# One written list of all steps, each with its own banks, in place of a list that repeats for each sequence

## The chip, the cores and the metric

The kernel runs on one core of one Trainium2 chip. The time is that of the device in microseconds, from one launch; of several runs the median is given. The core's engines are TensorE (PE, with its weight loads as PEld), VectorE (DVE), ScalarE (ACT), GpSimd (POOL) and SyncE (SP), which only issues DMAs here. Each works through its own queue in order, and they meet at semaphores.

## The reference

One layer of a hybrid network on 16 sequences of 256 tokens with 128 channels, in fp32. Four blocks follow one another, each on the normalised x and added to it:

```python
x = x + attn_a(_layernorm(x), ...)   # gated linear attention with decays by level, 32 heads of 64
x = x + ffn(_layernorm(x), ...)      # softmax attention, 16 heads of 8, then 8 experts of 256, the best 2 weighted
x = x + attn_b(_layernorm(x), ...)   # 9 sigmoid gates times v, shifted by 0, +-1, +-4, +-16, +-32 tokens
x = x + ffn(_layernorm(x), ...)      # the same weights as above
```

In attn_a an input projection gives z, x, B, C and small gates; a causal convolution of four taps and a silu follow; then `att = qk * decay * lam_ts`, where the level of a pair of tokens comes from a Fenwick tree; then the sum over tokens, the product with silu(z), an RMS norm and the output projection. No step of one sequence needs anything of another.

## The kernel before

All work is cut into steps. A step is a name, a layer (0, or 1 for the second ffn and the mixing block), a sequence n and a number k. The names in the order of one sequence: `gates` (layernorm, small gates, their running sums, the table of decays written to DRAM), `lvl` (39 loads that bring this table back), `conv`, `tap`, `taps`, `silu`, `xt`, `xcopy` (convolution: matmul, ACT's tap, DVE's three taps, silu, transposition, copy), `zgate`, `zact`, `qk`, `place`, `coef`; for each of eight units `weigh` (PE's log decays), `wexp` (their exponential on ACT), `prod` (times qk on DVE), `own` (POOL), `sum` (PE) and `gated` (DVE); `ssq` and `outp` (RMS and output projection). Then `fn`, `q`, `v`, `mload`, `smax`, `rowmax`, `maxt` (maxima of the scores, for which q and k are split in bf16 parts on POOL and go through DRAM), `sload`, `es`, `exps`, `ep`, `ocopy`, `tail` (scores, softmax, output, layernorm, expert choice), `up`, `relu`, `down`, `acc`, `experts` (the experts), `mix` (attn_b, k from 0 to 12), and `fn` to `experts` once more as layer 1.

The order is written by hand as text. `PERIOD` is one list of words, such as `up1.0+4@67`: step up, layer 1, k = 0, of the sequence that entered 4 turns ago, with PSUM banks 6 and 7. `order()` runs through the list once per turn, with 20 turns in all, so that up to five sequences are in work at once, and leaves out the sequences that don't exist; that is the fill in the first turns and the drain in the last. `build()` goes through the resulting list once per engine, in the blocks `sync`, `tensor`, `scalar`, `vector` and `gpsimd`; each takes the steps in which it has a part, in the order of the list, and waits on semaphores for what others must have done. A bank that is used again is waited for by the number of drains so far (`drained`), a filled one by `filled`; both numbers are counted from the list. So only the order within each engine counts, and what an engine does ahead of a step it doesn't take part in is of no account.

`order()` also sets ScalarE's tables. It walks the list of all steps and puts in a table load where the set changes:

```python
needed = ("silu_set" if what in SILU_SET else "exp_set" if step in EXP_SET.get(what, ()) else held)
if needed != held:
    hops.append((needed, 0, n, 0))
    held = needed
```

`SILU_SET` is silu, zact and mix; `EXP_SET` is some steps of gates, tail and outp, and all of wexp and exps. It goes by names, also for steps in which ACT has no part, such as `mix` 0 and `mix` 12 (k == NG + 3), which are VectorE's alone.

Lines that the text below names: L524 and L533 (SP: decay table out and back), L593 to L610 (gates on PE), L630 (conv and zgate), L653 (xt), L670 and L678 (weigh), L691 and L699 (sum), L710 (ssq), L724 (outp), L739 (fn), L765 (smax), L775 (maxt), L862 (up), L874 (down), L882 to L901 (mix), L916 and L918 (the table loads), L1003 (wexp), L1049 (exps), L1220 (taps), L1247 (prod), L1255 (gated), L1260 (w_out times norm_w, once, in the first sequence), L1295 (rowmax), L1379 (acc).

Of the kernel before, what the change touches and what calls it, by code (L numbers as in the profile page):

```python
# [122 lines left out]
PERIOD = """  # L123
up0.2+3@03 relu0.3+3 silu0.1+1 load_x0.0+0 ocopy1.3+4 up0.3+3@51 lvl0.0+1 lvl0.1+1 down0.2+3@7 experts1.3+5
conv0.2+1@32 ep1.3+4@4 conv0.3+1@65 down0.3+3@1 tap0.3+1 fn0.1+2@7 acc0.1+3 gates0.0+0 up0.5+3@34 acc0.2+3 xt0.0+1@7
silu0.2+1 conv0.4+1@13 taps0.2+1 acc0.3+3 taps0.3+1 relu0.5+3 up0.4+3@20 xcopy0.0+1 tap0.4+1 down0.5+3@7 lvl0.2+1
taps0.4+1 relu0.4+3 lvl0.3+1 lvl0.4+1 lvl0.5+1 tail1.0+4@54 xt0.1+1@2 xcopy0.1+1 q0.1+2@0 down0.4+3@6 acc0.4+3
tap0.5+1 conv0.5+1@24 relu0.6+3 up0.6+3@15 acc0.5+3 relu0.7+3 silu0.3+1 taps0.5+1 acc0.6+3 up0.7+3@61 q0.0+2@0
down0.6+3@3 down0.7+3@2 tail1.1+4@6 acc0.7+3 experts0.2+3 zgate0.0+1@71 tail1.2+4@0 silu0.4+1 v0.0+2@6 experts0.3+3
xt0.3+1@3 zact0.0+1 zgate0.6+1@05 zgate0.2+1@74 mix1.0+3 lvl0.6+1 xcopy0.3+1 zact0.6+1 zact0.2+1 silu0.5+1 tail1.3+4  # L130
xt0.2+1@2 conv0.6+1@75 xt0.4+1@0 conv0.7+1@43 mload0.0+2 tap0.6+1 xcopy0.2+1 xcopy0.4+1 tap0.7+1 mix1.1+3@12 taps0.6+1
place0.0+1@1 tail1.4+4@0 taps0.7+1 mix1.2+3@6 bcp0.0+1 mix1.3+3@2 mix1.4+3@5 mix1.5+3@1 rowmax0.0+2 zact0.5+1
zgate0.5+1@60 qk0.0+1@7 silu0.6+1 smax0.0+2@1524 mix1.6+3@3 qkc0.0+1 zact0.4+1 zgate0.4+1@01 mix1.7+3@6 tail1.5+4@3
rowmax0.1+2 smax0.1+2@7265 tail1.6+4 mix1.8+3@4 silu0.7+1 relu1.0+4 zact0.3+1 zgate0.3+1@30 mix1.9+3@1 taps0.8+1
up1.0+4@67 conv0.8+1@42 tap0.8+1 mix1.10+3@1 zgate0.7+1@06 zact0.7+1 xcopy0.6+1 rowmax0.2+2 xt0.6+1@7 experts1.0+4@5
zgate0.1+1@16 sload0.0+2 zact0.1+1 smax0.2+2@5740 lvl0.7+1 up1.1+4@16 relu1.1+4 experts1.1+4@2 mix1.11+3@7 rowmax0.3+2
xt0.5+1@5 xcopy0.5+1 down1.0+4@4 silu0.8+1 mix1.12+3 wexp0.0+1 smax0.3+2@3671 weigh0.0+1@02 wexp0.3+1 down1.1+4@5
weigh0.3+1@63 relu1.2+4 xt0.7+1@0 up1.2+4@27 maxt0.0+2@1 up1.3+4@32 gates0.1+0@7 down1.2+4@1 fn1.0+3 acc1.0+4
relu1.3+4 xcopy0.7+1 own0.0+1 acc1.1+4 wexp0.2+1 coef0.0+1 wexp0.1+1 exps0.0+2 prod0.0+1 weigh0.2+1@46 acc1.2+4
weigh0.1+1@25 gates0.2+0@37 es0.0+2@6412 sum0.0+1@0 fn1.1+3@7 prod0.1+1 own0.1+1 sum0.1+1@5 weigh0.4+1@3210 gated0.0+1  # L140
wexp0.4+1 ep0.0+2@6 own0.2+1 ocopy0.0+2 own0.3+1 own0.4+1 q1.0+3@4 es0.1+2@2571 exps0.1+2 own0.5+1 sum0.2+1@3 q1.1+3@0
up1.4+4@25 ep0.1+2@6 relu1.4+4 es0.2+2@0753 ocopy0.1+2 exps0.2+2 wexp0.5+1 mload1.0+3 sum0.3+1@2 prod0.2+1 gated0.1+1
weigh0.5+1@4615 own0.6+1 ep0.2+2@0 prod0.3+1 sload1.0+3 prod0.4+1 es0.3+2@3624 down1.3+4@7 own0.7+1 sum0.4+1@1
gated0.2+1 ocopy0.2+2 weigh0.6+1@5746 gates0.3+0 exps0.3+2 gated0.3+1 wexp0.6+1 prod0.5+1 acc1.3+4 ep0.3+2@2
down1.4+4@3 gates0.4+0@5 gates0.6+0 ocopy0.3+2 acc1.4+4 sum0.5+1@7 wexp0.7+1 weigh0.7+1@3065 gated0.4+1 prod0.6+1
gated0.5+1 tail0.0+2@24 up1.5+4@10 sum0.6+1@7 gates0.5+0 relu1.5+4 smax1.0+3@2563 prod0.7+1 tail0.1+2@4 sum0.7+1@0
gated0.6+1 rowmax1.0+3 cpart0.0+0 up1.6+4@27 tail0.2+2@4 smax1.1+3@1256 relu1.6+4 outp0.0+1@7 smax1.2+3@5146
ssq0.0+1@2 gated0.7+1 ssq0.1+1 ssq0.2+1 ssq0.3+1 smax1.3+3@0351 rowmax1.1+3 outp0.1+1 tail0.3+2 rowmax1.2+3
rowmax1.3+3 maxt1.0+3@6 tail0.4+2@4 acc1.5+4 outp0.2+1 down1.5+4@5 up0.0+2@40 down1.6+4@3 acc1.6+4 relu0.0+2 exps1.0+3
v1.0+3@2 fn0.0+1 relu1.7+4 es1.0+3@6137 up1.7+4@50 tail0.5+2@6 ep1.0+3@1 tail0.6+2 es1.1+3@6524 acc1.7+4 down1.7+4@3  # L150
exps1.1+3 conv0.0+0@05 tap0.0+0 taps0.0+0 up0.1+2@62 taps0.1+0 ocopy1.0+3 experts0.0+2@4 relu0.1+2 conv0.1+0@31
ep1.1+3@7 es1.2+3@4520 tap0.1+0 down0.1+2@6 ocopy1.1+3 experts0.1+2@7 ep1.2+3@5 es1.3+3@0712 exps1.2+3 experts1.2+4
ocopy1.2+3 exps1.3+3 acc0.0+2 relu0.2+2 down0.0+2@4 silu0.0+0 tap0.2+0
"""


START = """
# [6 lines left out]
def hop_words(text):  # L164
    for word in text.split():
        name, rest = word.split(".")
        step, n = rest.split("@")[0].split("+")
        yield name[:-1], int(name[-1]), int(step), int(n)


def hop_banks(text):
    for word in text.split():
        name, rest = word.split(".")
        if "@" in rest:
            yield (name[:-1], int(name[-1]), int(rest.split("+")[0])), tuple(int(b) for b in rest.split("@")[1])
# [1406 lines left out]
```

## Time and profile before

| | |
|---|---|
| median of 3 runs | 2107.03 us (2103.94 to 2107.87) |
| the profiled execution | 2103.15 us |
| its span, first to last instruction | 2101.4 us |
| PE, DVE, ACT, POOL busy | 1921.0, 1738.5, 1488.0, 775.6 us |
| mean granted TensorE clock | 0.966 of full speed |
| DMA | 117.14 MB, mean 56 GB/s |

The rows below come from that one execution, whose own time lies 3.9 us under the median of the three runs. A busy PE is not PE at its peak, since the ends of matmuls are modelled; an fp32 matmul shows as two records, and a weight load (PEld) runs beside the matmuls. "Idle before" is the time in which an engine had nothing running ahead of an instruction, with the engine, tile and line whose semaphore came last.

### The profile page before, as it was taken

How to read it: one execution, taken by the hardware profiler on the slowest of the kernel's cores; microseconds unless marked ns; L12 is line 12 of the kernel's file. 1: busy time of each engine (PE TensorE's matmuls, PEld its weight loads, DVE VectorE, ACT ScalarE, POOL GpSimd, SP SyncE). 2: the span in 40 equal slices, each digit the busy share in tenths (PEclk: the TensorE clock that was granted, in tenths of full speed). 3: DMA queues.
4: the chain of work that ended last, by engine and by line, in shares of the span. 5: the costliest groups of instructions: out<-in, count | busy, mean ns of one | idle time of the engine just before them, and what ended most of it. 6: DMA issues, size and time to landing. Idle time of an engine off the chain costs nothing.

```text
span 2101.4 us, 48245 instructions
## 1 busy us (share of the span) xinstructions
PE 1921.0 (91%) x16928; PEld 1491.0 (71%) x16928; DVE 1738.5 (83%) x4463; ACT 1488.0 (71%) x3207; POOL 775.6 (37%) x1139
## 2 busy tenths in 40 slices
PE   4779899999999999999999999999999999997757
PEld 3556677777877777786877778786777778774545
DVE  5776988989898988989898998989898898865643
ACT  4566768778686868778686877868686877855332
POOL 5313353525243343525244352424334352423120
PEclk8889999999999999999999999999999999998867
DMA  5021232211222222211222222121222221112110
GB/s 162 12 63 12 60 67 60 65 41 46 50 59 67 62 67 63 56 35 51 59 60 67 62 64 56 45 44 54 67 60 67 62 63 38 50 53 71 27 56 6
DMA packets 224576, 117.14 MB, mean 56 GB/s; under 512 B 124360, under 2 KB 210512, under 8 KB 219216
## 3 DMA queue, kind: packets, MB, share of 16 engines
q1 hardware_dynamic: 224336, 114.06, 21.5%
q8 instruction: 137, 2.24, 0.5%
q14 instruction: 103, 0.84, 0.1%
HBM read 67.60 MB, written 46.14 MB: 54 GB/s over the span
## 4 chain that ended last, share of the span: by engine, by line
PE 64%; DVE 23%; ACT 4%; issue 4%; SPq 2%; POOL 2%; DMA 1%; DVEq 0%; ACTq 0%; POOLq 0%
DVE nmax L1295 6%; PE psA L862 6%; PE psB L724 6%; DVE work L1220 5%; PE psB L874 5%; PE psA L874 5%; PE psA L699 5%; PE psB L803 3%; PE psB L862 3%; PE psA L630 3%; PE psB L699 2%; PE psA L803 2%; DVE att L1247 2%; DVE hid L1408 2%; PE psA L788 2%
## 5 line engine op out<-in xcount | busy, mean ns | idle before, releaser
L1247 DVE TENSOR_TENSOR att<-att,QK 128x1024 f32<-128x1024 f32 x192 | 251.2, 1341 | 15.2 <-ACT att L1003 15.1
L1529 POOL TENSOR_TENSOR own<-X,ccoef 128x512 f32<-128x512 f32 x128 | 160.2, 1257 | 206.7 <-PE psA L699 97.1
L1437 POOL TENSOR_SCALAR var_eps<-lnmv 128x2 f32<-128x2 f32 x128 | 40.4, 316 | 524.0 <-DVE lnmv L1110 521.3
L1220 DVE SCALAR_TENSOR_TENSOR work<-psA,c_conv_w,work 128x255 f32<-128x255 f32 (+2 forms) x450 | 195.4, 474 | 11.8 <-ACT work L961 11.8
L630 PE MATMUL psA<-xnT_a,c_w_in 128*128 128x256 f32 x608 | 177.9, 397 | 17.8 <-DVE hid L1220 8.7
L1072 ACT ACTIVATE hid<-psA,c_b 128x256 f32<-128x256 f32 x295 | 135.8, 485 | 79.4 <-PE psA L862 79.2
L1295 DVE TENSOR_REDUCE nmax<-psB 128x2 f32<-128x512 f32 x288 | 186.6, 680 | 1.1 <-PE psB L765 1.1
L862 PE MATMUL psA<-x1T,c_w 128*128 128x256 f32 x608 | 178.9, 394 | 1.5 <-DVE nmax L1295 1.3
L1049 ACT ACTIVATE pt<-psB 128x512 f32<-128x512 f32 x256 | 147.4, 614 | 31.5 <-PE psB L789 31.4
L1295 DVE TENSOR_REDUCE nmax<-psA 128x2 f32<-128x512 f32 x224 | 149.8, 681 | 15.1 <-PE psA L765 14.9
L1220 DVE SCALAR_TENSOR_TENSOR work<-psB,c_conv_w,work 128x255 f32<-128x255 f32 (+1 forms) x360 | 159.0, 474 | 2.7 <-ACT work L961 2.1
L874 PE MATMUL psB<-c_w,hid 128*128 128x128 f32 x1152 | 160.6, 285 | 0.4 <-ACT hid L1072 0.4
L874 PEld LDWEIGHTS psB<-c_w,hid 128*128 128x128 f32 x1152 | 148.3, 199 | 8.8 <-issue 4.2
L1519 POOL TENSOR_TENSOR O_sb<-O_sb,hid 128x256 f32<-128x256 f32 x128 | 98.8, 772 | 148.8 <-DVE hid L1408 141.6
L1049 ACT ACTIVATE pt<-psA 128x512 f32<-128x512 f32 x256 | 150.3, 618 | 0.1
L1379 DVE SCALAR_TENSOR_TENSOR ff<-psB,w_e,ff 128x128 f32<-128x128 f32 x288 | 86.8, 342 | 73.1 <-PE psB L874 71.4
L630 PE MATMUL psB<-xnT_a,c_w_in 128*128 128x256 f32 x480 | 137.9, 392 | 0.8 <-ACT hid L1072 0.7
L862 PE MATMUL psB<-x1T,c_w 128*128 128x256 f32 x416 | 125.3, 396 | 13.0 <-DVE nmax L1295 11.9
L630 PEld LDWEIGHTS psA<-xnT_a,c_w_in 128*128 128x128 f32 x608 | 107.3, 196 | 39.6 <-DVE hid L1220 10.3
L1003 ACT ACTIVATE att<-psA 128x512 f32<-128x512 f32 x176 | 96.6, 599 | 53.4 <-PE psA L670 51.9
L1003 ACT ACTIVATE att<-psB 128x512 f32<-128x512 f32 x208 | 114.9, 603 | 21.6 <-PE psB L670 18.8
L724 PE MATMUL psB<-c_w_out,Z 128*128 128x128 f32 x1024 | 124.3, 280 | 3.8 <-DVE c_w_out L1260 3.8
(326 smaller groups left out, 5375.3 us busy)
## 6 DMA issues: line engine op xcount, KB each, us to landing
qk_scr<-kparts SPq DMA_DIRECT2D x96, 192.0 KB, 2.4
k_stack<-qk_scr SPq DMA_DIRECT2D x32, 576.0 KB
q_stack<-qk_scr SPq DMA_DIRECT2D x32, 576.0 KB
qk_scr<-qparts SPq DMA_DIRECT2D x96, 128.0 KB, 1.9
k_max<-qk_scr SPq DMA_DIRECT2D x128, 64.0 KB, 2.0
q_max<-qk_scr SPq DMA_DIRECT2D x128, 64.0 KB, 2.0
lvl_scr<-work SPq DMA_DIRECT2D x32, 192.0 KB, 5.7
qk_scr<-qparts SPq DMA_DIRECT2D x96, 64.0 KB, 1.7
```

Source lines behind the costliest of these rows:

```text
L630: e.matmul(t[:, 0:T], w_in[:, first + j * P:first + (j + 1) * P], xnT_a[:, :], start=True, stop=True).then_inc(filled[b], 1)
L699: m = e.matmul(t[j * HD:(j + 1) * HD, f * P:(f + 1) * P], X[:, s, fc + j * HD:fc + (j + 1) * HD], att[:, 2 * f + j, :], start=False, stop= ...
L724: m = e.matmul(t[:, k * P:(k + 1) * P], Z[:, f, k * P:(k + 1) * P], w_out[:, f, :], start=(f == 0), stop=(f == NF - 1))
L862: e.matmul(t[:, 0:T], w_1[:, k, j * P:(j + 1) * P], x1T_b[lay][:, :], start=True, stop=True).then_inc(filled[b], 1)
L874: m = e.matmul(t[:, i * P:(i + 1) * P], hb[:, j, i * P:(i + 1) * P], w_2[:, 2 * k + j, :], start=(j == 0), stop=(j == 1))
L1003: e.activation(att[:, :, c:c + 64], t[:, :].rearrange("p (t h) -> p h t", h=HG), ACT.Exp).then_inc(drained[b], 1)
L1049: e.activation(pt_b[a % PTS][:, :, :].rearrange("p h q -> p (h q)"), t[:, :], ACT.Exp, scale=float(AD) ** -0.5).then_inc(drained[b], 1)
L1072: e.activation(hid_b[lay][k % 2][:, j, :], t[:, 0:T], ACT.Relu, bias=b_1[:, 2 * k + j:2 * k + j + 1]).then_inc(drained[b], 1)
L1220: m = e.scalar_tensor_tensor(out=cv[:, back:], in0=t[:, 0:T - back], scalar=conv_w[:, c, tap:tap + 1], in1=cv[:, back:], op0=ALU.mult, op1 ...
L1247: e.tensor_tensor(att[:, :, :], att[:, :, :], bc(QK[:, kq, :], 1, HG), ALU.mult).then_inc(att_done, 1)
L1295: e.tensor_reduce(nmax[:, i, p0:p0 + 2], t[:, :].rearrange("p (h k) -> p h k", k=T), AX.X, ALU.max).then_inc(drained[b], 1)
L1529: e.tensor_tensor(own_b[k % 2][:, :].rearrange("p (h c) -> p h c", c=HD), X[:, tt, h0 * HD:(h0 + HG) * HD].rearrange("p (h c) -> p h c", c ...
```

## The change

`PERIOD` and the empty `START` are replaced by `ORDER`, a text of all steps of all sequences in one order, each word with its sequence and its own banks. `order()` no longer unrolls turns; it reads the words and puts in the table loads by the same rule as before. The order within each engine is another one from place to place, in all turns, and so are the banks. Five waits are added for what the old order had made certain: PE ahead of the output projection (the gated sums of this half of the tokens), PE ahead of the first `up` of a layer (its input, transposed x1), DVE ahead of a gated sum (both gate tiles), DVE ahead of `rowmax` (the maxima of the layer before are taken) and POOL ahead of `own` (both copied tiles). No instruction of the computation is another one.

```diff
-PERIOD = """
-up0.2+3@03 relu0.3+3 silu0.1+1 load_x0.0+0 ocopy1.3+4 up0.3+3@51 lvl0.0+1 lvl0.1+1 down0.2+3@7 experts1.3+5
...
-"""
-START = """
-"""
+ORDER = """
+load_x0.0.0 gates0.0.0 gates0.1.0@0 gates0.2.0@12 conv0.0.0@34 gates0.3.0 tap0.0.0 gates0.4.0@5 gates0.5.0 taps0.0.0 conv0.2.0@67 cpart0.0.0
...
+wexp0.0.8 down1.0.5@3 xcopy0.7.8 weigh0.3.8@21 xt0.7.8@7 relu1.2.5 rowmax0.3.7 mix1.12.6 up1.2.5@56 up1.3.5@74 wexp0.3.8 maxt0.0.7@5 relu1.3.5
...
+"""
 def hop_words(text):
     for word in text.split():
-        name, rest = word.split(".")
-        step, n = rest.split("@")[0].split("+")
-        yield name[:-1], int(name[-1]), int(step), int(n)
+        name, step, rest = word.split(".")
+        n, _, used = rest.partition("@")
+        yield (name[:-1], int(name[-1]), int(n), int(step)), tuple(int(b) for b in used)
-def hop_banks(text):
...
 def order():
-    period = list(hop_words(PERIOD))
...
-    for turn in range(BATCH + max(lag for _, _, _, lag in period)):
-        runs += [(what, lay, turn - lag, step) for what, lay, step, lag in period
-                 if 0 <= turn - lag < BATCH and (what, lay, turn - lag, step) not in ahead]
     hops, held = [], "exp_set"
-    for what, lay, n, step in runs:
+    for hop, _ in hop_words(ORDER):
+        what, _, n, step = hop
         needed = ("silu_set" if what in SILU_SET else "exp_set" if step in EXP_SET.get(what, ()) else held)
...
+        first_up = {}
+        for hop in hops:
+            if hop[0] == "up":
+                first_up.setdefault(hop[1:3], hop)
...
 PE, outp, k < NT
+                    e.wait_ge(*empty(("sum", 0, n, NU // 2 * (k + 1) - 1)))
 PE, up
+                    if hop == first_up[lay, n]:
+                        e.wait_ge(*empty(("tail", lay, n, 4)))
 DVE, gated, tt == 0
+                        e.wait_ge(*empty(("zgate", 0, n, 2 * hg), 1))
 DVE, rowmax
+                    if nth[hop]:
+                        e.wait_ge(nmax_ready, nth[hop])
 POOL, own, tt == 0
+                        e.wait_ge(*empty(("xt", 0, n, 2 * hg)))
```

## Rows read from the trace of the kernel before

**Rows 1.** The page, part 1: busy us, share of the span and instructions of each engine.

```profile
PE 1921.0 (91%) x16928; PEld 1491.0 (71%) x16928; DVE 1738.5 (83%) x4463; ACT 1488.0 (71%) x3207; POOL 775.6 (37%) x1139
```

**Rows 2.** Windows: busy us (instructions) of PE, PEld, DVE, ACT, POOL; PEclk; DMA share; GB/s.

```profile
0.00:68.00 68.00, 34.90 (x144) 24.99 (x144) 40.68 (x106) 36.27 (x70) 31.01 (x40) 0.88 0.45 128
68.00:158.00 90.00, 67.97 (x554) 51.38 (x552) 68.53 (x147) 51.14 (x99) 22.59 (x33) 0.86 0.18 41
...
969.00:1000.00 31.00, 30.89 (x338) 21.91 (x337) 28.59 (x51) 28.42 (x60) 19.44 (x19) 1.00 0.10 30
1000.00:1020.00 20.00, 19.57 (x244) 15.63 (x244) 19.13 (x37) 9.28 (x18) 7.75 (x17) 1.00 0.57 123
974.00:1094.00 120.00, 116.42 (x1064) 91.78 (x1063) 108.02 (x280) 92.56 (x201) 47.76 (x72) 1.00 0.22 57
1811.00:1930.00 119.00, 106.40 (x965) 79.97 (x963) 78.28 (x201) 69.31 (x151) 39.56 (x56) 0.91 0.18 51
1930.00:2050.00 120.00, 81.11 (x549) 59.01 (x548) 59.75 (x175) 44.03 (x99) 25.11 (x42) 0.80 0.18 50
```

**Rows 3.** PE's waits, 497 to 1691 us: engine line waited for: total us, times, longest us.

```profile
PE psA L888 <- ACT srcT L1077: 14.1, 10, 1.4
PE psB L862 <- DVE nmax L1295: 7.7, 10, 0.8
PE psA L893 <- ACT hid L1091: 7.1, 10, 0.7
PE psB L691 <- DVE Z L1255: 4.3, 10, 0.4
```

**Rows 4.** PE's waits, 0 to 68 us.

```profile
PE psA L630 <- DVE hid L1220: 8.7, 2, 5.3
PE psB L608 <- DVE work L1194: 5.9, 1, 5.9
PE psA L670 <- DMA high<-lvl_scr: 3.1, 1, 3.1
```

**Rows 5.** PE's waits, 68 to 158 us.

```profile
PE psA L630 <- DVE work L1220: 5.2, 1, 5.2
PE psB L608 <- DVE work L1194: 3.9, 1, 3.9
PE psB L724 <- DVE c_w_out L1260: 3.8, 1, 3.8
PE psA L765 <- DMA q_max<-qk_scr: 3.1, 1, 3.1
```

**Rows 6.** Timeline, 100 to 127 us: start, us, what, [idle before <- releaser].

```profile
115.13 0.35 DVE L1266 SCALAR_TENSOR_TENSOR x<-psB,rms,x 128x128 f32<-128x128 f32 x1 [11.53 <-ACT rms L1023]
...
121.60 2.07 PE L630 MATMUL psA<-xnT_a,c_w_in 128*128 128x256 f32 x4 [5.20 <-DVE work L1220]
```

**Rows 7.** ACT's groups: xcount | busy us, mean ns | idle before.

```profile
L918 ACT ACT_TABLE_LOAD x33 | 42.3, 1283 | 0.6
L916 ACT ACT_TABLE_LOAD x33 | 42.3, 1283 | 0.6
```

**Rows 8.** Timeline of ACT, 954 to 975 us.

```profile
956.38 1.28 ACT L916 ACT_TABLE_LOAD   x1
957.76 0.22 ACT L1061 ACTIVATE gate_e<-gate_l 128x16 f32<-128x16 f32 x1
957.99 1.28 ACT L918 ACT_TABLE_LOAD   x1
```

**Rows 9.** PE's waits, 1930 to 2101 us.

```profile
PE psA L765 <- DMA q_max<-qk_scr: 10.5, 2, 9.0
PE psB L765 <- DVE nmax L1295: 6.6, 6, 2.1
PE psB L775 <- DVE nmax_bf L1302: 6.6, 2, 3.3
```

**Rows 10.** All waits, the whole span.

```profile
PEld psA L699 <- issue: 13.4, 80, 0.2
```

More of the change, by code:

```diff
@@ L129 @@
[L129 to L138, printed above, removed]
@@ new lines @@
+weigh0.7.7@1574 own0.7.7 down1.4.4@0 tail0.0.6@36 wexp0.7.7 prod0.7.7 up1.5.4@15 sum0.6.7@7 relu1.5.4 gates0.5.8 smax1.0.5@4036 tail0.1.6@1
+rowmax1.0.5 gated0.5.7 gated0.6.7 cpart0.0.8 sum0.7.7@5 tail0.2.6@1 smax1.1.5@4036 up1.6.4@27 outp0.0.7@1 smax1.2.5@5403 gates0.6.8 ssq0.0.7@6
+gated0.7.7 ssq0.1.7 ssq0.2.7 relu1.6.4 ssq0.3.7 rowmax1.1.5 tail0.3.6 smax1.3.5@2754 lvl0.0.8 rowmax1.2.5 outp0.1.7 rowmax1.3.5 tail0.4.6@0
+maxt1.0.5@3 outp0.2.7 relu0.0.6 lvl0.1.8 acc1.5.4 fn0.0.7 exps1.0.5 v1.0.5@2 down1.6.4@7 up0.0.6@54 down1.5.4@6 es1.0.5@0315 tail0.5.6@4 up1.7.4@60
@@ new lines @@
+tail0.5.11@4 exps1.1.10 ep1.0.10@3 ocopy1.0.10 es1.1.10@5704 tap0.0.13 relu0.0.11 down1.7.9@2 tail0.6.11 conv0.0.13@57 relu0.1.11 up0.1.11@04
+ep1.1.10@3 acc1.7.9 experts0.0.11@2 taps0.0.13 conv0.1.13@61 ocopy1.1.10 down0.1.11@0 es1.2.10@4253 tap0.1.13 exps1.2.10 taps0.1.13 experts1.2.9
+lvl0.3.13 experts0.1.11@7 es1.3.10@4265 exps1.3.10 acc0.0.11 relu0.2.11 ep1.2.10@1 down0.0.11@3 tap0.2.13 ocopy1.2.10 silu0.0.13 gates0.0.14
+up0.2.11@42 silu0.1.13 conv0.2.13@76 conv0.3.13@53 acc0.1.11 down0.2.11@4 up0.3.11@20 experts1.3.9 relu0.3.11 ep1.3.10@1 xt0.0.13@7 tap0.3.13
@@ new lines @@
+tap0.6.13 zgate0.0.13@25 zact0.2.13 zgate0.6.13@43 tail1.3.10 silu0.5.13 zgate0.2.13@02 conv0.7.13@50 tap0.7.13 mload0.0.12 mix1.1.11@22
+zgate0.4.13@61 zact0.6.13 taps0.6.13 tail1.4.10@2 xcopy0.3.13 taps0.7.13 mix1.2.11@4 mix1.3.11@3 xt0.4.13@2 xcopy0.4.13 lvl0.5.13 mix1.4.11@7
+bcp0.0.13 mix1.5.11@4 zact0.5.13 zgate0.5.13@53 silu0.6.13 rowmax0.0.12 smax0.0.12@0274 mix1.6.11@5 mix1.7.11@3 zact0.4.13 silu0.7.13 zact0.3.13
+zgate0.3.13@05 smax0.1.12@3267 tail1.5.10@1 lvl0.6.13 rowmax0.1.12 xt0.6.13@4 tail1.6.10 up1.0.10@01 mix1.8.11@5 qk0.0.13@3 relu1.0.10 mix1.9.11@2
@@ new lines @@
+smax1.0.13@7164 gated0.7.15 sum0.7.15@3 smax1.1.13@5027 rowmax1.1.13 tail0.1.14@1 up1.6.12@64 tail0.2.14@1 v1.0.13@3 outp0.0.15@5 smax1.2.13@6402
+relu1.6.12 ssq0.0.15@7 own0.7.15 tail0.3.14 ssq0.1.15 rowmax1.2.13 sload1.0.13 ssq0.2.15 ssq0.3.15 smax1.3.13@1364 rowmax1.3.13 outp0.1.15
+tail0.4.14@0 maxt1.0.13@2 relu0.0.14 outp0.2.15 down1.5.12@1 up0.0.14@36 acc1.5.12 exps1.0.13 relu1.7.12 tail0.5.14@4 down1.6.12@7 es1.0.13@0251
+up1.7.12@36 exps1.1.13 fn0.0.15 es1.1.13@4072 ep1.0.13@5 up0.1.14@13 acc1.6.12 tail0.6.14 down1.7.12@6 experts0.0.14@4 ep1.1.13@0 fn0.1.15@7
@@ L165, in hop_words @@
     for word in text.split():
-        name, rest = word.split(".")
-        step, n = rest.split("@")[0].split("+")
-        yield name[:-1], int(name[-1]), int(step), int(n)
-def hop_banks(text):
[L172 to L175, printed above, removed]
-def order():
-    period = list(hop_words(PERIOD))
-    runs = [(what, lay, n, step) for what, lay, step, n in hop_words(START) if n < BATCH]
-    ahead = set(runs)
-    for turn in range(BATCH + max(lag for _, _, _, lag in period)):
-        runs += [(what, lay, turn - lag, step) for what, lay, step, lag in period
-                 if 0 <= turn - lag < BATCH and (what, lay, turn - lag, step) not in ahead]
+        name, step, rest = word.split(".")
+        n, _, used = rest.partition("@")
+        yield (name[:-1], int(name[-1]), int(n), int(step)), tuple(int(b) for b in used)
+def order():
     hops, held = [], "exp_set"
-    for what, lay, n, step in runs:
+    for hop, _ in hop_words(ORDER):
+        what, _, n, step = hop
         needed = ("silu_set" if what in SILU_SET else "exp_set" if step in EXP_SET.get(what, ()) else held)
@@ L190, in order @@
             held = needed
-        hops.append((what, lay, n, step))
+        hops.append(hop)
     return hops
@@ L197, in build @@
     hops = order()
-    banks = dict(hop_banks(PERIOD))
+    banks = dict(hop_words(ORDER))
     bank_at, nth, uses, seen_hops = {}, {}, [0] * 8, {}
     for hop in hops:
-        for j, b in enumerate(banks.get((hop[0], hop[1], hop[3]), ())):
+        for j, b in enumerate(banks.get(hop, ())):
             bank_at[hop, j] = (b, uses[b])
```

385 lines of the change are left out of this document (366 added, 19 removed).

## The prediction, made before the changed kernel ran

> **What bounds the kernel now.** I read the busy times first: PE works 1921 us of 2101, DVE 1738, ACT 1488 [rows 1]. A share over the whole span hides that the program has three stretches, so next comes the table of windows, cut where a new sequence enters the pipeline [rows 2]. In the middle, from about 377 to 1811 us, a new sequence enters every 119 to 120 us, 12 times; in the turn at 974 to 1094 us PE is busy 116.42 of 120 us at full clock, DVE 108.02, ACT 92.56. While the pipeline fills, PE is busy 34.90 of 68 us and 67.97 of 90 us, with a granted clock of 0.88 and 0.86. While it drains, PE is busy 106.40 of 119 and 81.11 of 120, at 0.91 and 0.80. So PE's own queue sets the time in the middle, and chains through several engines set it at both ends.
>
> Then PE's waits, stretch by stretch. In the ten turns from 497 to 1691 us they sum to 33 us in four rows: 1.4 us in each turn inside the first matmul of the mixing stage (a transpose, ACT's copy, the next matmul, all in one step), 0.8 us for a bank held by a row maximum, 0.7 us for a tanh, 0.4 us for a gated sum [rows 3]. The 1.4 us lie within one step, and no order of steps removes them. What another order can remove is 3.6 - 1.4, some 2.2 us a turn, 26 us over 12 turns. In the fill it is 8.7 us for bank drains by the convolution taps, 5.9 us for the gates and 3.1 us for the decay table [rows 4]; then 5.2, 3.9, 3.8 and 3.1 us in the second stretch [rows 5]. The last two sequences pay 10.5 us for the loads of q_max and 6.6 and 6.6 us for row maxima [rows 9].
>
> **What the change is, by counting in the two lists.** The steps are the same 4928 (16 times the 308 words of the period), with 3840 bank uses in both, so every engine runs the same instructions apart from ACT's table loads. It is no new pipeline: the PE work listed ahead of each stage of each sequence is moved by 1.2 us on average and by 18 at most, the lists weighed with the trace's PE durations. On each engine steps have moved by 1.5 places on average on PE (at most 26, of 2288), 1.7 on ACT, 0.8 on DVE, 0.4 on GpSimd, 1.1 on SP. Nearly every bank is another one: 163 of 2224 steps that use banks keep theirs.
>
> **Fill: -9 us.** The first 65 us don't shrink. The first decay tile waits for 39 loads that SP issues one after another, and PE waits for the last of them 3.1 us [rows 4]; the taps' 8.7 us and the gates' 5.9 us lie ahead of that wait, so filling them with later gate matmuls, as the list does, moves no end. But two steps of PE that stood behind the wait (a transpose and the next sequence's first) now stand ahead of it, some 1.8 us less afterwards. From 68 to 158 us the list acts on things that wait. Of the next sequence's convolution, two pairs are now ahead of the output projection, where PE idles 3.8 us until DVE has scaled w_out [rows 5], and one group of taps is ahead of DVE's output step, where DVE idles 11.53 us for the rms [rows 6]. That group is six instructions of 0.47 us, 2.4 us, and it comes off DVE's queue behind 115 us, where PE waits 5.20 us for the group that follows it [rows 6]. The running sum for the next sequence's gates stands one gated sum later in DVE's queue and one sum later in PE's, which takes up part of the 3.9 us [rows 5]. I take 2 us before 68, 6 of the 16 us of waits up to 158, and 1 from the following turns together. Bounds: 0 and 18.
>
> **Middle: -5 us.** The bank that the first expert matmul of the second layer takes was last used by a row maximum (0.8 us a turn [rows 3]); in the new list both of its banks come from other kinds of step in 9 of 16 turns, and the sum that waited for the gated sum ahead of it takes another kind's bank in 14. Against that, 2061 new banks and some 115 PE steps moved by more than 5 places bring waits of their own where a reuse is now closer. I take a net gain of 0.4 us a turn times 12, of the 2.2 that are there. Bounds: -26 us if they all go, and +18 us if each turn gains 1.5 us of new waits, as much as the two largest removable ones of rows 3 together.
>
> **Table loads: 0 on the path, 38.5 us of ACT.** The program that reads the list puts a load of the silu set ahead of each step named mix, and step 12 of mix is one, though only DVE has work in it. In the old list it stands ahead of the first exponential of the decay tiles. In the new one it stands behind it, for 14 sequences, and once more at the end: ACT then loads silu and, right after, exp again for nothing. Counted with the program's rule that is 96 loads in place of 66. A load is 1283 ns [rows 7], and the step behind it starts 0.1 us after its end: 956.38 + 1.28 = 957.66 against 957.76 [rows 8]. A pair therefore costs 2.57 us, 15 pairs 38.5 us. Queued behind a pair are three exponentials, two relus, then the first softmax exponentials and the gates' own, for which DVE's products and PE's sums wait. ACT is busy 28.42 of 31 us from 969 to 1000 us and 9.28 of 20 after [rows 2]: 2.58 us of idle time in the tight part, about one pair, and 10.7 us behind it. So a pair is worked off before the next sequence's stages, and I take 0; at most it is 2.57 us in each turn.
>
> The Trainium skill speaks against such an order: "ScalarE: Activation LUTs", Rules for kernel authors, says to do all of one table set before switching, and What ACT_TABLE_LOAD costs puts a switch at 1283 ns for the load and 1380 ns for a drain, 2.66 us. The trace agrees with the load and not with the drain, which these rows don't show. By the page's price the 30 loads would be an estimated 80 us of ACT in place of 38.5, and its idle time could not hide that.
>
> **The five waits: +1 us.** PE waits for two gated sums ahead of the output projection (32 instructions) and for the transposed x1 ahead of the first expert matmul of a layer (32). Behind each waits all of PE's queue; both were done before by the order. DVE's wait for the maxima of the layer before, DVE's second wait on the gate tiles and GpSimd's on the copied x are for things done on the same queue or pairs of the same stage. What a wait costs where it is long fulfilled, no row shows by itself. The nearest is the weight load that starts late with nothing to wait for, 13.4 us for 80, 0.17 us each [rows 10]: 64 of them would be 11 us. The matmuls ahead still run then, so nothing is the other end; I take 1 us, nearer to that end.
>
> **Drain: -6 us.** The longest wait, 9.0 us for q_max [rows 9], is a chain of GpSimd's splits and DMAs. The new list starts k ahead of q and puts about as much expert work in between as before, so most of it stays; 1 us. Behind it, in the score matmuls and ahead of the transposition of the maxima, PE waits 6.6 and 6.6 us [rows 9]; there the list puts a down step more for sequence 14, an up and a down step for 15, and I take 3 of the 13 us. In the last 36 us four up steps stand ahead of the expert weights' transposition, which fills the gap there, 2 us. Bounds: 0 and 20.
>
> **The sum.** -9 - 5 + 0 + 1 - 6 = -19 us. The profiled run took 2103.15 us, its span is 2101.4; 2103.15 - 19 = 2084. The median of the runs, 2107.03, lies 3.9 us above the profiled run, so I name 2088 for a median.
>
> **The rivals.**
> ACT's table loads decide (slower). Place: between the first and second exponential group of each turn, where ACT has 2.58 us to spare in 31 us and DVE 2.4 [rows 2]. If the idle time lies ahead of what waits and not behind it, each pair is paid in full: 14 times 2.57 is 36 us, less about 15 of the gains above, 2107 + 21 = 2128; paid by half, 2110. It decides from the point where a pair is delayed by more than what PE still has queued ahead of the sums, under 2 us. For it: three engines over 90% busy there. Against it: the idle time behind. The skill's rule on grouping by table set is this case.
> New waits by banks eat the gain: 1.5 us in 12 turns is 18 us, 2107. For it: DVE has 12 us a turn to spare, so a late step is not soon made up. The order does what it says and the time stands still.
> The list removes nearly all it can: 26 in the middle, 14 in the fill, 10 in the drain, 2057. Against it: most of the ends are chains of one sequence, which no order shortens.
> The list does not act at all, since the ends were bound by DMAs and the middle by PE's work: 2107 with 3 us either way.
>
> **How the numbers follow.** Forecast 0.50 (2070 to 2100), nearly all removed 0.16 (2057), new bank waits 0.13 (2100 to 2115), table loads 0.16 (2108 to 2128), no effect 0.05. Faster takes the first two, 0.66; within 0.2%, about what a measurement of this kernel tells from no change, 0.10 from the bank waits and no effect; slower 0.24. The range 2050 to 2125 leaves out the far ends of the two outer cases.
>
> **What the new profile would show.** 96 table loads, two with no activation in between behind the first exponentials. PE idle of 68 to 158 us down from 22 to about 16; the wait of 5.2 us gone. PE's waits in a middle turn at 2 to 4 us, with other releasers than row maxima. If a new sequence enters every 119 us and the ends are each some 7 us shorter, the steps are right. If the turn is over 120.5 us and PE waits for the exponentials of the decay tiles or DVE's products, the table loads were underrated. If the waits are spread over many banks, it is the second rival. Wrong it would be above all by the middle, where 1 us a turn counts for 12.

## The result, and the profile of the changed kernel

| | before | after |
|---|---|---|
| median of the runs | 2105.49 us (4 runs, 2103.29 to 2107.87) | 2136.39 us (4 runs, 2126.58 to 2142.73) |
| ratio | | 1.0141, 95% interval 1.0120 to 1.0162: slower |
| profiled execution, its span | 2103.15, 2101.4 us | 2126.58, 2124.8 us |

The forecast was 2088 us and faster. The time is 2136 us, slower, and above the range of 2050 to 2125. The profiled execution of after is the fastest of its four, so the rows below show 23 us of loss (2124.8 against 2101.4) and not the 31 us of the medians.

The first part of the page, and the row of TensorE's granted clock over 40 slices of the span, answer to [rows 1]:

```profile
PE 1942.0 (91%) x16928; PEld 1496.2 (70%) x16928; DVE 1747.3 (82%) x4463; ACT 1517.3 (71%) x3237; POOL 792.0 (37%) x1139
PEclk9899999999999999999999999999999999998987
```

ACT has 30 instructions more, the table loads, and is busy 29.3 us longer. PE has the same 16928 matmuls and is busy 21 us longer. That is the first thing to explain: where the same matmuls take longer, the clock is the suspect. Over the whole span it can't be, for the mean granted clock is 0.971 in this execution and 0.966 in that of before; in single stretches it can. The windows (columns as in [rows 2]): the stretch from the second to the third sequence, the same 90 us as in [rows 2], two turns of the middle, and the last but one stretch of 120 us:

```profile
59.00:151.00 92.00, 73.59 (x584) 51.72 (x584) 71.33 (x158) 59.65 (x116) 22.57 (x35) 0.89 0.19 42
68.00:158.00 90.00, 75.31 (x618) 53.45 (x618) 74.40 (x155) 59.39 (x115) 24.26 (x36) 0.91 0.19 41
981.00:1105.00 124.00, 119.03 (x1068) 92.89 (x1068) 108.98 (x280) 95.71 (x206) 47.81 (x70) 0.99 0.22 54
1105.00:1231.00 126.00, 119.30 (x1068) 93.47 (x1068) 111.32 (x286) 97.35 (x208) 53.02 (x74) 0.99 0.23 55
1959.00:2079.00 120.00, 86.12 (x584) 61.17 (x582) 59.78 (x182) 48.60 (x109) 26.20 (x43) 0.85 0.18 50
```

A turn takes 124 and 126 us where it took 120, and its clock is 0.99 where it was 1.00. To see where the time comes from I mark one matmul, the first of each sequence's gates, and note its start in both traces (us):

| sequence | 1 | 2 | 3 | 5 | 7 | 9 | 11 | 13 | 15 | mixing stage of 15 |
|---|---|---|---|---|---|---|---|---|---|---|
| before | 68 | 158 | 260 | 497 | 736 | 974 | 1213 | 1453 | 1691 | 1993 |
| after | 59 | 151 | 251 | 496 | 737 | 981 | 1231 | 1480 | 1722 | 2028 |

The fill gains 9 us by the fourth sequence (number 3), as forecast. The mark of sequence 1 (59 against 68) shows no gain by itself: the new list puts this step ahead of the first decay tile, and that tile starts at 66.1 us against 65.4. Then 40 us are lost in the middle, in turns of 119.5 to 127.6 us that were all 119.4 to 119.8. From the mixing stage of the last sequence to the end the new list gains again.

PE's waits from 496 to 1722 us, ten turns like those of [rows 3], the six largest:

```profile
PE psA L1234 <- ACT srcT L1423: 10.7, 7, 2.2
PE psA L951 <- DVE work L1540: 5.0, 4, 1.6
PE psB L951 <- DVE work L1540: 4.9, 5, 1.3
PE psB L1234 <- ACT srcT L1423: 3.5, 3, 1.6
PE psA L1132 <- DMA q_stack<-maxT: 2.6, 2, 1.9
PE psA L1220 <- ACT att L1349: 2.2, 1, 2.2
```

The in-step wait of the mixing stage is still there (10.7 + 3.5 us, line 1234 is 888 of before). The row maximum of [rows 3] (7.7 us) is gone, as is the gated sum (4.3). New are the fourth gate step (L951, 9.9 us in nine turns), a DMA, and waits for `att`, the exponentials of the decay tiles. One of the latter, in the timelines of ACT and PE (start, us, what, [idle before <- releaser]), and the clock right behind it:

```profile
979.77 1.01 ACT L1418 ACTIVATE hid<-psB,c_b 128x256 f32<-128x256 f32 x2
980.80 1.28 ACT L1264 ACT_TABLE_LOAD   x1
982.09 1.28 ACT L1262 ACT_TABLE_LOAD   x1
983.38 1.08 ACT L1349 ACTIVATE att<-psA 128x512 f32<-128x512 f32 x2
984.03 1.16 PE L1220 MATMUL psA<-c_w,hid 128*128 128x128 f32 x8 [2.23 <-ACT att L1349]
985.70:989.10 3.40, 3.40 (x16) 1.71 (x13) 0.51 (x2) 2.06 (x4) 0.34 (x1) 0.50 0.01 2
```

Two loads with nothing between them, the exponential behind them, and an expert matmul that waits 2.23 us because its bank is drained by that exponential. Then the granted clock is 0.50, the lower of its two levels (1.2 GHz), for 3.4 us in which PE is busy all the time. Such a stretch at half the clock does 1.7 us of work in 3.4. Before shows none between 275 and 1790 us; after shows five of 3.4 us and one of 6.8 in the middle. So there are three suspects for the middle: the 15 pairs of loads, waits of the new order or its banks, and the clock behind either.

### The profile page after: what moved, and what is told of

It is laid out like the page before. It is cut to its first block and busy times, and to the rows that moved or that the text cites. A ratio compares the mean times of both kernels' runs of the same rounds, so it can differ in the third digit from the quotient of the medians.

```text
span 2124.8 us, 48449 instructions
## 1 busy us (share of the span) xinstructions
PE 1942.0 (91%) x16928; PEld 1496.2 (70%) x16928; DVE 1747.3 (82%) x4463; ACT 1517.3 (71%) x3237; POOL 792.0 (37%) x1139
## 5 line engine op out<-in xcount | busy, mean ns | idle before, releaser
L1593 DVE TENSOR_TENSOR att<-att,QK 128x1024 f32<-128x1024 f32 x192 | 262.8, 1403 | 21.8 <-ACT att L1349 20.8
L1566 DVE SCALAR_TENSOR_TENSOR work<-psA,c_conv_w,work 128x253 f32<-128x253 f32 (+2 forms) x414 | 185.3, 474 | 11.6 <-ACT work L1307 11.2
L1566 DVE SCALAR_TENSOR_TENSOR work<-psB,c_conv_w,work 128x253 f32<-128x253 f32 (+2 forms) x396 | 177.4, 473 | 5.7 <-ACT work L1307 5.5
L1208 PE MATMUL psB<-x1T,c_w 128*128 128x256 f32 x518 | 152.9, 396 | 3.2 <-ACT att L1349 1.9
L1418 ACT ACTIVATE hid<-psB,c_b 128x256 f32<-128x256 f32 x251 | 116.6, 484 | 52.3 <-PE psB L1208 43.9
L1208 PE MATMUL psA<-x1T,c_w 128*128 128x256 f32 x506 | 146.7, 391 | 2.7 <-ACT att L1349 1.2
L1220 PE MATMUL psA<-c_w,hid 128*128 128x128 f32 x1024 | 144.1, 286 | 5.4 <-ACT att L1349 2.2
L1220 PEld LDWEIGHTS psA<-c_w,hid 128*128 128x128 f32 x1024 | 131.3, 198 | 18.6 <-issue 8.7
L1418 ACT ACTIVATE hid<-psA,c_b 128x256 f32<-128x256 f32 x245 | 113.5, 488 | 41.6 <-PE psA L1208 36.7
L1220 PE MATMUL psB<-c_w,hid 128*128 128x128 f32 x1024 | 140.5, 282 | 1.3 <-ACT hid L1418 1.3
L1220 PEld LDWEIGHTS psB<-c_w,hid 128*128 128x128 f32 x1024 | 129.3, 195 | 13.2 <-issue 7.6
```

Source lines behind the costliest of these rows:

```text
L1208: e.matmul(t[:, 0:T], w_1[:, k, j * P:(j + 1) * P], x1T_b[lay][:, :], start=True, stop=True).then_inc(filled[b], 1)
L1220: m = e.matmul(t[:, i * P:(i + 1) * P], hb[:, j, i * P:(i + 1) * P], w_2[:, 2 * k + j, :], start=(j == 0), stop=(j == 1))
L1418: e.activation(hid_b[lay][k % 2][:, j, :], t[:, 0:T], ACT.Relu, bias=b_1[:, 2 * k + j:2 * k + j + 1]).then_inc(drained[b], 1)
L1566: m = e.scalar_tensor_tensor(out=cv[:, back:], in0=t[:, 0:T - back], scalar=conv_w[:, c, tap:tap + 1], in1=cv[:, back:], op0=ALU.mult, op1 ...
L1593: e.tensor_tensor(att[:, :, :], att[:, :, :], bc(QK[:, kq, :], 1, HG), ALU.mult).then_inc(att_done, 1)
```

## The experiments

In all of them the ratio is against runs of the kernel before on the same chip. A sequence's turn is the time from the first gate matmul of one sequence to that of the next.

**The list as it is, without the needless loads.**

```diff
-        needed = ("silu_set" if what in SILU_SET else ...
+        needed = (held if (what, step) in (("mix", 0), ("mix", NG + 3)) else "silu_set" if what in SILU_SET else ...
```

> The changed kernel with its list, banks and waits as they are, but the steps mix.0 and mix.12 no longer ask for a table set: 66 table loads in place of 96. If the 15 pairs are paid on the path (14 times 2.57 us and the clock drops behind them), the time falls by 30 to 45 us, to about 2095 to 2106 us. If the order of the steps and the banks are what costs, ACT is 38 us less busy and the time moves by under 5 us, 2130 to 2140. In between, each pair costs the share of 2.57 us that the difference gives when divided by 14.

Measured: 2105.28 us, ratio 0.9998 (0.9987 to 1.0009). ACT's loads are 33 and 33 again:

```profile
L1264 ACT ACT_TABLE_LOAD x33 | 42.3, 1283 | 0.6
L1262 ACT ACT_TABLE_LOAD x33 | 42.3, 1283 | 0.6
```

The pairs are 30 of the 31 us, some 2.0 us each. What is left is no gain either: the new list without its loads is as fast as the old one within 0.1%, though its ends are shorter. So the middle loses by something else as well.

**The old list with the same loads added.**

```diff
         hops.append((what, lay, n, step))
+        if (what, lay, step) == ("wexp", 0, 0) and n >= 2 or (what, lay, n, step) == ("exps", 0, BATCH - 1, 0):
+            hops += [("silu_set", 0, max(n - 2, 0), 0), ("exp_set", 0, n, 0)]
```

> The kernel before with the same 15 pairs of table loads (silu, then exp) behind the first exponential of the decay tiles of sequences 2 to 15 and once in the drain, and nothing else changed: 96 loads. If the pairs make the changed kernel slow, this one is slow too, 2135 to 2145 us. If they are hidden, as the prediction had it, 2103 to 2108 us and PE's waits in the middle are the same 3.6 us a turn.

This kernel and the two behind it also have the edit of the first run, which leaves the 66 loads of the old list at 66.

Measured: 2151.05 us, ratio 1.0214 (1.0200 to 1.0228), 45 us for 38.5 us of loads, more than was expected. From sequence 5 on the turns are 123.2 to 123.6 us, but for one of 122.5 and two of 121.5 and 121.6. This kernel shows the mechanism undisturbed, since all else is as before. PE's waits, 503 to 1732 us; ACT and PE around one pair; and the windows (columns as in [rows 2]) ahead of and behind PE's wait:

```profile
PE psA L864 <- ACT att L1005: 20.3, 10, 2.1
PE psA L890 <- ACT srcT L1079: 14.0, 10, 1.4
PE psB L864 <- DVE nmax L1297: 7.7, 10, 0.8
PE psA L895 <- ACT hid L1093: 7.0, 10, 0.7
PE psB L693 <- DVE Z L1257: 4.3, 10, 0.4
```

```profile
988.37 1.09 ACT L1005 ACTIVATE att<-psA 128x512 f32<-128x512 f32 x2
989.48 1.28 ACT L920 ACT_TABLE_LOAD   x1
990.76 1.28 ACT L918 ACT_TABLE_LOAD   x1
992.06 0.60 ACT L1005 ACTIVATE att<-psB 128x512 f32<-128x512 f32 x1
992.55 0.59 ACT L1005 ACTIVATE att<-psA 128x512 f32<-128x512 f32 x1
993.20 1.74 PE L864 MATMUL psA<-x1T,c_w 128*128 128x256 f32 x4 [2.05 <-ACT att L1005]
```

```profile
987.00:990.00 3.00, 2.90 (x33) 1.95 (x26) 3.00 (x7) 2.95 (x5) 1.08 (x2) 1.00 0.02 5
993.60:997.00 3.40, 3.40 (x14) 2.86 (x14) 1.07 (x1) 2.10 (x6) 2.90 (x2) 0.50 0.01 2
```

Each of the ten turns has one new wait of 2.05 us (in one turn 1.83), and all others are those of [rows 3] within 0.1 us. The matmul that waits, the up step 3 of layer 1, takes the bank that the second exponential group drains. In before that group ended at 972.95 and the matmul started at 973.36 us, 0.41 us later:

```profile
971.86 0.60 ACT L1003 ACTIVATE att<-psB 128x512 f32<-128x512 f32 x1
972.35 0.59 ACT L1003 ACTIVATE att<-psA 128x512 f32<-128x512 f32 x1
973.36 1.13 PE L862 MATMUL psA<-x1T,c_w 128*128 128x256 f32 x4
```

A pair delays the group by 2.57 us, less 0.41 is 2.16, measured 2.05. Another bank would have shortened this wait and not removed it: when PE stops at 991.15 us all eight are taken by the order of the list, and the first of them (bank 4) comes free at 992.31, when DVE has added up an expert's product, 0.89 us before PE resumes. That is why ACT's idle time, which begins 30 us later, is of no use: PE runs ahead of ACT by eight banks and no further. Then comes the clock: PE resumes at 993.20, and from 993.6 to 997.0 it is granted 0.50. There are ten such drops in the middle for twelve such waits. The two turns that have none, 121.5 and 121.6 us, lie 2.1 us above before's, the turns with one about 3.8: a drop adds some 1.75 us.

**Half of a pair in the same place.**

```diff
-            hops += [("silu_set", 0, max(n - 2, 0), 0), ("exp_set", 0, n, 0)]
+            hops.append(("exp_set", 0, n, 0))
```

> The kernel before with one needless load (exp again, 1.28 us) in place of the pair at the place where the pair cost 3.9 us a turn: behind the first exponential of the decay tiles. There the pair made PE wait 2.05 us for a bank, and a drop of the clock followed that took 1.75 us more. If the wait grows one for one with the load and the clock drops only behind the longer wait, it is 1.28 - 0.5 = 0.8 us a turn, 11 us, 2117 us (2113 to 2120) with no drops in the middle. If the cost is in proportion to the loads, half of 45 us, 2128 us.

Measured: 2117.32 us, ratio 1.0053 (1.0041 to 1.0066), 11.6 us, and a granted clock of 1.00 from 498 to 1701 us. PE's waits there, the first two:

```profile
PE psA L890 <- ACT srcT L1079: 14.1, 10, 1.4
PE psA L864 <- ACT att L1005: 8.2, 11, 0.8
```

Half of the loads cost a quarter, 11.6 against 45 us. Of each delay some 0.4 us are free and the rest is paid one for one; behind the longer wait of 2.05 us the clock mostly fell as well, so that one was paid nearly twice.

**The same pairs in another place.**

```diff
+        if (what, lay, step) == ("outp", 0, 1) and n >= 1:
+            hops += [("silu_set", 0, n, 0), ("exp_set", 0, n, 0)]
         hops.append((what, lay, n, step))
```

> The kernel before with the same number of needless pairs (15, 96 loads), but ahead of the exponential-set step of the output projection, where ACT idles 3.96 us in a turn of the trace of before (1019.3 to 1023.3 us). If it is the place that decides, a pair of 2.57 us fits in and the time is that of before, 2103 to 2109 us. If ACT's total of busy time decides, 38.5 us more wherever it lies, it is 2140 to 2151 us like the run with the pairs behind the first exponential.

Measured: 2105.14 us, ratio 0.9995 (0.9986 to 1.0004): nothing, with ACT busy 1526.7 us against 1488. ACT's timeline shows the pair and 1.38 us of idle time still left behind it, ahead of the rms step that waits for PE:

```profile
1021.01 1.28 ACT L920 ACT_TABLE_LOAD   x1
1022.30 1.28 ACT L918 ACT_TABLE_LOAD   x1
1024.95 0.26 ACT L1023 ACTIVATE rms<-psA,eps_col 128x2 f32<-128x2 f32 x1 [1.38 <-PE psA L734]
```

**The new ends around the old middle, and the reverse.** The cuts lie where both lists have named the same set of steps; the first is shown:

```diff
 weigh0.1.2@20 coef0.0.2 wexp0.1.2 prod0.0.2 exps0.0.1
-own0.1.2 gates0.2.3@35 es0.0.1@7146 sum0.0.2@2
+gates0.2.3@37 es0.0.1@6412 sum0.0.2@0 fn1.1.0@7
...
```

> The new list and banks for the first 499 steps (up to about 160 us) and the last 463, the old order with the old banks for the 3966 steps between, in the new form with the five waits; 70 table loads. If the gains of both ends (7 to 9 us in the fill, about 7 in the drain) are the ends' own, the middle enters a sequence every 119.4 us as before and the time is 2089 to 2094 us. If the fill's lead is lost whatever the middle is, since the pipeline settles at the same place, 2096 to 2100. If the five waits cost much in the middle, 2100 or more.

Measured: 2089.71 us, ratio 0.9922 (0.9910 to 0.9935), faster than both kernels. Its turns in the middle are 119.5 to 119.7 us (one of 120.8), with no drop of the clock.

> The reverse of the run before it: the old order and banks for the first 499 and the last 463 steps, the new order and banks between; 92 table loads. If the new middle costs 40 us by itself, 2140 to 2150 us, with turns of 119 to 127 us. If the lost time is that the lead from the new fill is given back (a middle that can only run at its own pace), 2110 to 2125.

Measured: 2151.95 us, ratio 1.0218 (1.0204 to 1.0231). So the loss is the new middle's own, 46 us with its 13 needless pairs, and the ends' gain is their own too. The two runs also add up: -0.78% and +2.18% give +1.40%, and the changed kernel has +1.41%.

**The new ends without their two needless pairs.** The edit is that of the first run, on the list with the new ends.

> The list with new ends and old middle (2089.7 us), with mix.0 and mix.12 asking for no table set: 66 loads in place of 70. Two pairs less, 5.1 us of ACT at the ends. If the pairs are paid there too, 2083 to 2087 us; if ACT has time to spare at the ends, 2088 to 2091.

Measured: 2082.85 us, ratio 0.9896 (0.9881 to 0.9911), the fastest kernel of all, 22.8 us below before. The two pairs at the ends were paid in full as well: 0.9922 less 0.9896 is 5.5 us. PE's waits at the end, 1921 to 2078 us, the largest and those that belong to [rows 9]:

```profile
PE psA L1109 <- DMA q_max<-qk_scr: 6.8, 1, 6.8
PE psB L1228 <- DVE src L1460: 4.7, 1, 4.7
...
PE psA L1119 <- DVE nmax_bf L1651: 2.4, 1, 2.4
...
PE psA L1220 <- DVE nmax L1644: 1.5, 1, 1.5
PE psB L1119 <- DVE nmax_bf L1651: 1.0, 1, 1.0
PE psA L1109 <- DVE nmax L1644: 0.6, 1, 0.6
PE psB L1109 <- DVE nmax L1644: 0.6, 3, 0.2
```

The three rows that held 23.7 us in [rows 9] hold 11.4 here: 6.8 for q_max, 3.4 for the maxima's transposition (L1119) and 1.2 for row maxima in the score matmuls (L1109). A down step (L1220) now waits 1.5 us for a row maximum.

**The fill alone.** The same cut, with all steps behind the first 499 in the old order.

> The new list for the first 499 steps alone, all else the old order and banks, with 66 loads. The run with both new ends gave 2082.9 us, 22.8 less than before; its sixteenth sequence's mixing stage starts 12 us earlier, so the fill should be worth 9 to 12 us and the drain the rest: 2094 to 2097 us. If the drain only worked since the fill came first, 2088 or less; if the lead is lost on the way, 2100.

Measured: 2097.23 us, ratio 0.9966 (0.9953 to 0.9978), 7.1 us. The run before it has the same list up to the last 463 steps, so the drain is 0.9966 less 0.9896, 14.7 us.

**The five waits alone.** The old order and banks, written out as one list of 4928 words, with the five waits.

> The old order with the old banks, written out as one list, and the five waits: the waits alone. If they cost what the prediction took, 2104 to 2108 us, with the middle turn at 119.4 us. If each costs 0.17 us on PE's queue, the other bound, 64 of them give 11 us, 2117.

Measured: 2106.16 us, ratio 1.0013 (1.0004 to 1.0021), 2.7 us. The turns are 118.9 to 119.8 us, as before's, and sequence 15 starts at 1691.5 us in both profiles; the 2.3 us by which this span is longer lie behind that. The run can't tell apart the five waits and the list as such.

**The gate step of the new middle, moved.** In the changed kernel without the loads the gate step k = 4 (L951) is what waits anew. First the whole step goes behind the next PE step, for sequences 3 to 15; one of the 13 places:

```diff
-gates0.4.8@4 gated0.4.7 sload1.0.5 ocopy0.3.6 prod0.6.7 sum0.5.7@2 acc1.4.4
+gated0.4.7 sload1.0.5 ocopy0.3.6 prod0.6.7 sum0.5.7@2 gates0.4.8@4 acc1.4.4
```

> The changed kernel with 66 table loads (as in the first of these runs, 2105 us) and one step moved: the fourth gate step of sequences 3 to 15 stands one PE step later (behind a gated sum's matmuls, an expert step or a decay tile), as in the old list, where it stood behind an expert step. It cost 0.6 to 1.6 us of waiting in 9 of 10 turns and two of the clock drops followed it. If these waits are what the new middle pays, the time falls by 9 to 15 us to 2090 to 2097. If the delayed step only passes its wait to what is behind it, since DVE is the one that is late, 2102 to 2107.

Measured: 2117.37 us, ratio 1.0057 (1.0044 to 1.0069), a miss: 12 us slower than with the step in its place. The timelines of DVE and PE at one of the places show what the move does:

```profile
885.79 1.21 DVE L1593 TENSOR_TENSOR att<-att,QK 128x1024 f32<-128x1024 f32 x1
886.93 1.66 DVE L1538 TENSOR_TENSOR SPL<-SPL,work 128x640 f32<-128x640 f32 x1
888.62 0.23 DVE L1540 TENSOR_TENSOR work<-SPL,c_neg_a 128x64 f32<-128x64 f32 x1
...
888.99 0.38 PE L951 MATMUL psB<-work,c_tri 128*128 128x32 f32 x2 [2.54 <-DVE work L1540]
```

The step also issues DVE's work (L1538, L1540), and that went back with it, behind one more product (L1593). PE's wait for it grew from 0.99 to 2.54 us in this turn, and a drop of the clock followed. But the time was lost elsewhere. This execution is 8 us longer than the profiled one without the move (2114.2 against 2106.3), and the ten turns from sequence 5 to 15 take 1211.4 us in both. The turn from sequence 3 to 4 takes 125.4 us against 117.9; there the step did not wait before, and now PE waits 4.38 us for it and is granted 0.50 for 10.2 us:

```profile
280.26 0.60 PE L951 MATMUL psB<-work,c_tri 128*128 128x32 f32 x2 [4.38 <-DVE work L1540]
```

So in the middle the moved step changed nothing in sum, and at one place where it had been on time it made PE wait. Then the other way round: the gate step stays, and an expert product goes ahead of it, which only PE executes.

```diff
-ep0.3.3@6 ocopy0.2.3 wexp0.6.4 prod0.5.4 gates0.4.5@3 down1.4.1@0
+ep0.3.3@6 ocopy0.2.3 wexp0.6.4 prod0.5.4 down1.4.1@0 gates0.4.5@3
```

> The changed kernel with 66 table loads (2105 us) and one PE step, the fifth down product of layer 1, moved to stand directly ahead of the fourth gate step of sequences 5, 11 and 13; in the other turns no bank is free at that place. The gate step's own DVE work keeps its place in DVE's queue, unlike in the run that moved the gate step itself and lost 12 us. If that was what lost, the waits of 0.96, 1.56 and 1.36 us in these turns go and one clock drop with them: 2098 to 2103 us. If the wait only moves on, 2104 to 2107, and if the old bank of the down product is missed elsewhere, more.

Measured: 2105.05 us, ratio 1.0003 (0.9994 to 1.0012), no gain. In the profiles turn 11 fell from 120.2 to 117.6 us, and turn 12 rose from 123.5 to 126.2. The largest wait of turn 12 in the run without the loads, and in this one:

```profile
PE psA L1132 <- DMA q_stack<-maxT: 1.7, 1, 1.7
```

```profile
PE psA L1132 <- DMA q_stack<-maxT: 2.8, 1, 2.8
```

The 2.6 us came back as 1.1 us more waiting for the transfer of the score maxima, and as a clock drop of 6.8 us (from 1453 us on) in place of one of 3.4 (at 1436). So some 1.1 us of the gates' wait had been cover for the transfer. Whether the other clock drop came of the move, one execution of each can't say: the two profiles also differ in drops where their lists are the same.

**A wait of the old middle, removed.** In the fastest list so far, 13 times:

```diff
-up1.0.5@67 conv0.8.8@42 tap0.8.8 mix1.10.6@1 zgate0.7.8@06
+up1.0.5@27 conv0.8.8@46 tap0.8.8 mix1.10.6@1 zgate0.7.8@02
```

> The fastest list so far (new ends, old middle, 66 loads, 2082.9 us) with two banks of three steps exchanged in each turn of the middle: the first up step of layer 1 takes bank 2 in place of 6, which a row maximum still holds (0.8 us of waiting a turn), the last convolution pair takes 6 in place of 2, and the gate product behind it 2 in place of 6. If waits add up as the prediction's term for the middle had it, 0.66 us a turn go, 8 us in all: 2074 to 2077. If ACT, without a pause there between its two table loads and the transposed gates, sets the time, the wait moves to the mixing product 3 us later, which then waits 1.3 to 1.5 us: 2081 to 2085.

Measured: 2088.59 us, ratio 0.9929 (0.9914 to 0.9943), some 6 us slower than without the exchange; neither forecast. PE's waits over ten turns:

```profile
PE psA L1239 <- ACT hid L1437: 9.4, 10, 0.9
PE psB L973 <- DVE work L1566: 5.6, 10, 0.6
...
PE psA L1208 <- DVE nmax L1644: 2.6, 10, 0.3
```

The row maximum's 8.6 us became 2.6, as meant. The mixing product's wait rose from 7.1 to 9.4, and a later one, zgate0.1, now waits 5.6 us for the taps that drain bank 6. The turn is 120.0 to 120.3 us, from 119.6. PE's idle time explains 2.2 of the 5.2 us in ten turns. In the other 3 us PE is busy longer with the same matmuls at a clock of 1.00 throughout; the cause stays open.

## Why the prediction was wrong

**Table loads: the step that failed.** The count was right, 96 and 66, and so was the price of a pair, 2.57 us. Wrong was "So a pair is worked off before the next sequence's stages, and I take 0". It set the loads against ACT's idle time from 1000 us on; what decides is the first that waits for the steps behind them. In the old order that is the bank of an expert matmul, and its slack was in the trace of before: 0.41 us. Pairs at a place with real idle time cost nothing. At their place they cost 30 us in the changed kernel (1.0141 to 0.9998), and 45 in the old order, 3.9 us a turn, so the bound "at most it is 2.57 us in each turn" failed too. In the changed kernel the same kind of wait is seen at 984 us; how the rest of its 30 us is made up is less clear. From sequence 5 to 15 the profiled execution is 15 us longer with the loads than without, 9 us of it PE's idle time (waits for `att` are 6 us of these) and 6 us longer busy. The rival named the mechanism and the point from which it decides, "under 2 us" of queued PE work, but its 2108 to 2128 had no term for the clock, and set 15 us of gains against it that the middle had already eaten. The Trainium skill, "ScalarE: Activation LUTs", Rules for kernel authors, was right to speak against the order. The drain of 1380 ns that its part What ACT_TABLE_LOAD costs adds to each switch is not seen here, and the measurement decides: the exponential starts at 983.38, and the second load ended at 982.09 + 1.28 = 983.37. Ahead of the first load, which starts at 980.80, the relu ends at 979.77 + 1.01 = 980.78.

**The clock: a term the prediction did not have.** Its sums took each wait once. With the old middle the clock fell to half for 3.4 us, at a cost of 1.75, behind ten of the twelve long waits of the run with pairs, and not once in the middle of the eight profiles whose longest wait there is 1.4 us. With the new middle this does not hold: of 25 waits of 1.8 us and more in its five profiles 15 have a drop beside or behind them, and some drops follow waits under 1 us. The clock accounts for part of the loss. From sequence 5 to 15 PE is busy 19 us longer in after than in before, and 20.5 us at half the clock are 10 of them; the other 9 stay open. At the ends it is the other way: over the whole span PE is busy at half the clock for 103 us in after and 104 in before.

**Middle: -5 us, was +22 without the loads.** The best list has old turns of 119.6 us, the new list without its loads 121.1 on average; from 2082.9 to 2105.3 us there are 22.4 us, of which the ten turns hold 15.8. The two steps of the prediction's argument came true: the row maximum's wait and the gated sum's went, and other banks' waits stayed small. (In the new list both banks come from other kinds of step in 8 turns of 16 and not in 9, and in two of these they do so in the old list too.) What came instead was data, not banks: 9.3 us for the gate step's DVE work and 2.8 for a transfer over ten turns. PE is idle 39 us against 37. Five drops of the clock add some 8.5. Some 5 us more PE is busy at the full clock; that part is measured but not explained. The second rival, new waits of banks at 1.5 us a turn, comes out at the right size, 1.6 us a turn, and that is luck: waits are 0.25 us of it, and they are waits for data. The sentence "What another order can remove is 3.6 - 1.4" was not borne out: the new list took both waits away and got others, and where one exchange of banks took 0.6 us of a wait away the turn grew longer.

**Fill: -9 us, right in size and in place.** The run of the fill alone gives 7.1 us. It differs from the run of the five waits alone only in the order and banks of the fill, so these give 1.0013 less 0.9966, 9.9 us. Ahead of 68 us almost nothing is won, where 2 us were forecast: the first decay tile starts 0.7 us later than before, and PE has started 146 matmuls by then against 144. From 68 to 158 us it is some 8 us, where 6 were forecast: PE's 697th matmul starts at 149.6 us against 158.2, and its idle time in this stretch is 14.7 us against 22.0 (about 16 were forecast). The wait of 5.2 us fell to 1.7 and did not go.

**Drain: -6 us, mis-sized.** It was 14.7. The waits fell where the prediction has its mechanism, expert steps of the last two sequences between the score matmuls; no run tests that by itself. The prediction took 3 of 13 us for the row maxima and 1 of 10.5 for q_max. [rows 9] gave back 8.6 of its 13.2 us for the maxima, of which 1.5 stand elsewhere now, and 3.7 for q_max. Of the 15 us by which the stretch behind the start of sequence 15 is shorter, 12 are idle time of PE and 3 busy time.

**Five waits: +1 us, right within its bounds.** 2.7 us, interval 1 to 4, for the waits and the written-out form together, and none of it in the middle turns.

**The account.** Fill and drain with the waits -22.8, the middle's order and its clock drops +22.4, the loads +30, together +30 of the 31 us measured. These runs build on one another, so this sum must come out; the two runs with ends and middle exchanged are the separate test of it.

## What to carry to other kernels

Cost a delay on an engine by the first thing that waits behind it, not by the engine's idle time: where engines are coupled by a small pool of buffers, the slack is what the buffers hold, here 0.41 us beside 10 us of idle time. In this balanced pipeline neither single wait that was removed from PE's queue made the kernel faster, and a part of one had been cover for a later wait. A step that is moved takes its work on every engine with it. Edits at the ends, where chains through several engines set the time, paid here; test them apart from the steady part, since a sum of both (here -23 and +52) hides what is worth keeping.

## What the runs showed of the hardware

I had not expected a wait on PE of about 2 us to cost nearly twice its length. In the old order with pairs, ten of twelve waits of 2 us were followed by 3.4 us at a granted clock of 0.50 (the two without are one of 2.06 and the one of 1.83 us), while 0.8 us (half a pair) and 1.4 us (the mixing stage, in each turn) never were. In the new order it is less regular. Without the loads, the drop at 757 us follows a wait of 1.53 us, that at 1190 one of 1.82 us, one at 1211 a wait of only 0.61 us, and a wait of 1.73 us at 1314 has none behind it. With the down product moved, waits of 2.61 us at 485 and 2.79 us at 1393 have none, and a drop at 726 us follows a wait of 0.32 us, in a turn whose longest wait is 0.61. What PE was doing ahead of these differs, and no run here separates it. After's runs also spread more than before's, 16 us against 5, at mean clocks of 0.959 to 0.971 and the longer the lower.
